# VectorE's block transposes in place of TensorE's six, and the norms' root parts moved into PSUM, in a sliding-window attention and binarised FFN block

## The reference

```python
q, k = l2norm(proj(Wq)), l2norm(proj(Wk))          # 16 heads of 16 channels, norms per head
v = proj(Wv)
attn = q @ k.T                                      # per head
rel = pos[None, :] - pos[:, None]                   # key minus query
mask = (rel < 0) | (rel >= 128)                     # a query sees itself and the next 127 keys
attn = softmax(where(mask, -1e30, attn - abs(rel) * slope[h]))
x = layernorm(x + (attn @ v) @ Wo.T)
h = gelu(x @ binarize(w1).T + b1)                   # 1024 hidden, weights = sign * row mean of |w|
x = layernorm(x + h @ binarize(w2).T + b2)
```

## Time and profile before

| | |
|---|---|
| median of 3 runs | 369.94 us (369.66 to 370.51) |
| span of the profiled execution | 368.4 us |
| PE (TensorE matmul) busy | 353.2 us, 96% |
| DVE (VectorE) busy | 308.7 us, 84% |
| ACT (ScalarE) busy | 307.3 us, 83% |
| POOL (GpSimd) busy | 285.4 us, 77% |
| PE, attention, 107.2 to 135.8 us | 28.60 of 28.60 us |
| granted TensorE clock | 0.997 of full speed over the span |

### The profile page before, as it was taken

One profiled execution on the slowest core, in us unless ns is written; L12 is line 12 of the kernel. 1 busy time (PEld: TensorE's weight loads), 2 busy tenths in 40 slices (PEclk: granted clock), 3 DMA queues, 4 the chain that ended last, 5 costly groups with the idle time before them and its releaser, 6 DMA issues. The chain is left out here.

```text
span 368.4 us, 13096 instructions
## 1 busy us (share of the span) xinstructions
PE 353.2 (96%) x4461; PEld 244.1 (66%) x4461; DVE 308.7 (84%) x771; ACT 307.3 (83%) x532; POOL 285.4 (77%) x440
## 2 busy tenths in 40 slices
PE   8789999999999999999999999999999999999992
PEld 5555676667766776776677677675666667667682
DVE  5977899898898898898899988879777887786775
ACT  3588888898898998898899999988888888887753
POOL 1188999889989999998999999757756856856433
PEclk9999999999999999999999999999999999999998
DMA  7678944744655646667767773303303513413113
GB/s 231 143 117 186 185 109 98 157 99 94 137 120 106 142 96 132 139 159 154 156 144 155 153 147 74 59 4 59 59 0 59 115 45 72 114 39 76 59 59 114
DMA packets 106884, 40.19 MB, mean 109 GB/s; under 512 B 92128, under 2 KB 105824, under 8 KB 106720
## 3 DMA queue, kind: packets, MB, share of 16 engines
q1 hardware_dynamic: 106848, 39.73, 49.6%
HBM read 12.72 MB, written 4.19 MB: 46 GB/s over the span
## 5 line engine op out<-in xcount | busy, mean ns | idle before, releaser
L1341 POOL TENSOR_SCALAR_AFFINE_SELECT prob<-prob 128x512 f32<-128x512 f32 x252 | 153.7, 646 | 11.1 <-ACT prob L700 11.1
L700 ACT ACTIVATE prob<-ps 128x1024 f32<-128x1024 f32 (+1 forms) x128 | 122.2, 1009 | 13.5 <-PE ps L390 13.4
L551 PE MATMUL ps<-yT,sgn 128*128 128x512 f16 x256 | 61.1, 379 | 0.0
L772 ACT ACTIVATE ps<-ps,bias,alpha 128x512 f32<-128x512 f32 x64 | 47.9, 750 | 15.6 <-PE ps L551 12.5
L421 PE MATMUL ps<-wqkv,xt 128*128 128x512 f32 x124 | 58.7, 596 | 1.2 <-DVE qkn L952 1.1
L411 PE MATMUL ps<-prob,vdiag 128*17 128x128 f32 x1024 | 51.3, 274 | 0.3
L411 PE MATMUL ps<-prob,vnext 128*17 128x128 f32 x992 | 49.9, 273 | 0.0
L1409 POOL TENSOR_TENSOR resid<-z,resid 128x256 f32 (+1 forms) x31 | 22.5, 726 | 29.9 <-DVE z L1173 29.9
L551 PEld LDWEIGHTS ps<-yT,sgn 128*128 128x128 f16 x256 | 25.0, 98 | 22.6
L390 PE MATMUL ps<-qkT 64*64 64x192 f16 (+2 forms) x1024 | 33.7, 248 | 2.8 <-DMA qkT<-parts 2.7
L454 PE MATMUL ps<-wo,oT 128*128 128x256 f32 x128 | 36.2, 405 | 0.1
(11 more groups left out here) (113 smaller groups left out, 690.2 us busy)
## 6 DMA issues: line engine op xcount, KB each, us to landing
xt<-in_xT SPq DMA_DIRECT2D x32, 128.0 KB, 2.1
resid<-in_x SPq DMA_DIRECT2D x32, 128.0 KB, 2.2
out_dram<-resid SPq DMA_DIRECT2D x7, 512.0 KB, 2.9
w<-in_w2T SPq DMA_DIRECT2D x1, 1024.0 KB, 7.7
w<-in_w1T SPq DMA_DIRECT2D x4, 256.0 KB, 3.3
w_nat<-in_w SPq DMA_DIRECT2D x4, 256.0 KB, 3.3
wqkv<-in_wqkvT SPq DMA_DIRECT2D x3, 256.0 KB, 3.9
qkT<-parts SPq DMA_TRANSPOSE x39, 4.3
```

Of the source, the lines that this page charges most:

```text
L551: mm = nc.tensor.matmul(ps[:, bank, :], sgn1[:, c, P * k:P * k + P], yT[:, par, a, c, :, :], start=(m == 0), stop=(m == 2 * DC - 1))
L700: nc.scalar.activation(to, scored, ACT.Exp, scale=QK_SCALE ** -2).then_inc(exp_done, 1)
L772: nc.scalar.activation(bank, bank, ACT.Gelu, bias=bias1[:, k:k + 1], scale=alpha1[:, k:k + 1]).then_inc(gelu_done, 1)
L1341: return nc.gpsimd.affine_select(out=at, in_=at, compare_op=ALU.is_ge, fill=0.0, base=-near, pattern=[[0, CH], [1 if near else -1, P]], ch ...
```

## The change

- TensorE's transposes L438 (four) and L445 (two) go, and so do ScalarE's two copies L674 and L680. In their place VectorE turns bank 7 in 32x32 blocks into `turned` in SBUF (`turn_sums`, 512 columns) at the very start of its step, takes the reciprocals and multiplies from `turned` (both inputs are now in SBUF), and turns the 256 columns of `otok` in 32x32 blocks into `oT` (`scale_sums`). The order of the rows of `Wo` is changed on the host to fit.
- `project_out` goes behind `project_qk`, writes to bank 7 and waits for `turn_sums` of the block after; `weighted_sum` waits for `add_output` of that result.
- The root's three temporaries lie in PSUM bank 1 beside the values, from step 4 on (`parts_in_psum`). `project_v` of the next block writes the same bank, so it waits for the Newton round.
- The seeds (L863) go behind `fade_values`. The two products of `fade_values` become one of 512 columns (`faded`).
- The doubling copy goes from VectorE to ScalarE, behind the root.
- GpSimd cuts two chunks at once: four instructions of 1024 columns in a step for eight of 512. The low halves stand between the two pairs.

```diff
+        faded = sb("faded", [P, 2, XS, H, HD + 1])
+        turned = sb("turned", [P, H, 2 * HD])
+        parts_in_psum = tuple(ps[:, VO, D + 64 * n:D + 64 * n + 2 * H + 1] for n in range(3))
...
             def weighted_sum(q, c, slot, near=True):
                 if c == 0:
                     pe.wait_ge(v_ready, q + 2 if near else NB)
-                    count(pe, ot_ready, q)
+                    count(pe, sums_turned, q)
+                    count(pe, resid_done, q - 1 if not isinstance(q, int) or q < NB - 2 else 0)
...
             def project_v(n, slot):
                 count(pe, v_ready, n)
-                count(pe, resid_done, n - 4)
+                if not isinstance(n, int) or 6 <= n < NB - 1:
+                    pe.wait_ge(newton, norm_base(n - 2, True) + NORM_OPS)
...
+            def project_out(q, par):
+                pe.wait_ge(ot_ready, q + 1)
+                pe.wait_ge(sums_turned, q + 2)
                 for k in range(DC):
-                    mm = nc.tensor.transpose(ps[:, OT, P * k:P * k + P], otok[:, P * k:P * k + P], id32[:])
-                mm.then_inc(ot_done, 1)
-            def project_out(q, values, added=0):
-                pe.wait_ge(ot_ready, q + 1)
-                pe.wait_ge(v_ready, values)
-                count(pe, resid_done, added)
-                for k in range(DC):
-                    mm = nc.tensor.matmul(ps[:, VO, D:2 * D], oT[:, k, :], wo[:, k, :],
+                    mm = nc.tensor.matmul(ps[:, OT, D * par:D * par + D], oT[:, par, k, :], wo[:, k, :],
                                           start=(k == 0), stop=(k == DC - 1))
                 mm.then_inc(wo_done, 1)
...
+            def turn_sums(q):
+                dve.wait_ge(pv_done, q + 1)
+                count(dve, onorm_done, q)
+                nc.vector.transpose(turned[:].rearrange("p b d -> p (b d)"), ps[:, OT, :]).then_inc(sums_turned, 1)
+            def scale_sums(q, par):
+                dve.wait_ge(sums_turned, q + 1)
+                nc.vector.reciprocal(rden[:], turned[:, :, HD]).then_inc(rden_done, 1)
+                dve.wait_ge(rden_done, q + 1)
+                count(dve, ot_ready, q)
+                nc.vector.tensor_tensor(otok[:].rearrange("p b a d -> p a b d"),
+                                        turned[:, :, 0:HD].rearrange("p (a b) d -> p a b d", a=2),
+                                        rden[:].rearrange("p (a b) -> p a b", a=2).unsqueeze(3).to_broadcast(
+                                            [P, 2, H // 2, HD]),
+                                        ALU.mult).then_inc(onorm_done, 1)
+                dve.wait_ge(onorm_done, q + 1)
+                count(dve, wo_done, q - 1)
+                nc.vector.transpose(oT[:, par].rearrange("p k t -> p (k t)"),
+                                    otok[:].rearrange("p b a d -> p (b a d)")).then_inc(ot_ready, 1)
...
-                for to, at in ((vdiag, 0), (vnext, 1)):
-                    made = nc.vector.tensor_tensor(to[:, slot, :, 0:HD], v,
-                                                   fade[:, at, :].unsqueeze(2).to_broadcast([P, H, HD]), ALU.mult)
-                made.then_inc(v_ready, 1)
+                nc.vector.tensor_tensor(faded[:, :, slot, :, 0:HD], v.unsqueeze(1).to_broadcast([P, 2, H, HD]),
+                                        fade[:].unsqueeze(3).to_broadcast([P, 2, H, HD]), ALU.mult).then_inc(v_ready, 1)
...
+            def double(n, par):
+                done = n + 1
+                if not isinstance(n, int):
+                    done = act.to_reg(done)
+                act.wait_ge(lo_done, done)
+                nc.scalar.activation(parts[:, par, 0:H, 2:4, :], parts[:, par, 0:H, 0:2, :],
+                                     ACT.Copy).then_inc(parts_ready, 1)
...
-                at = prob[:, NEAR_AT[slot % 2] if near else OWN_AT[slot], CH * c:CH * c + CH, :]
+                at = prob[:, NEAR_AT[slot % 2] if near else OWN_AT[slot], 2 * CH * pair:2 * CH * pair + 2 * CH, :]
                 return nc.gpsimd.affine_select(out=at, in_=at, compare_op=ALU.is_ge, fill=0.0, base=-near,
-                                               pattern=[[0, CH], [1 if near else -1, P]],
+                                               pattern=[[0, 2 * CH], [1 if near else -1, P]],
                                                channel_multiplier=-1 if near else 1)
```

252 lines of the change are left out of this document (112 added, 140 removed).

## The result

| | before | after |
|---|---|---|
| median of the runs, us | 370.23 (369.66 to 372.72, 4 runs) | 376.27 (375.39 to 378.12, 4 runs) |
| ratio | | 1.016, 95% interval 1.012 to 1.020 |
| span of the profiled execution, us | 368.4 | 374.4 |
| mean granted clock | 0.997 | 0.974 |
| PE, DVE, ACT, POOL busy, us | 353.2, 308.7, 307.3, 285.4 | 339.0, 310.9, 293.5, 268.9 |

The kernel became slower by 6.0 us. The forecast was 356.3, and its range ended at 365.2. Here and in the experiments, runs more than 1.5% above the fastest of the same kernel are left out of the medians. TensorE is busy for 14.2 us less, where the forecast's terms for it add to 20.8 (32 x 0.65), and it stands idle for 20.2 us more (35.4 against 15.2). The page of the kernel after says where: its lines 2 are the busy tenths in 40 slices of 9.4 us.

The account below looks back on a forecast made before the run. TensorE's own work was taken to bound the attention step at 7.15 us, three engines close behind. Loop -12.5, edges -2.6 and tail +1.5 gave -13.6 us, a median of 356.3 us; range 349.0 to 365.2.

Parts of the forecast that it names:

- rival (d): VectorE's block transposes cost twice the rate per column; its step becomes 7.40 us, the kernel slower at 380.1 us; 8%.
- rival (b): GpSimd's wide cuts save nothing, 1.24 us each; the round is 6.98 and the time 364.5 us; 12%.
- `otok`'s wait: On VectorE, otok now reads both inputs from SBUF and may wait for a cut: 0.31 us taken, bounds 0 and 1.05.
- rival (c): On VectorE, otok waits about 0.67 us on average behind longer cuts; VectorE's sum is 6.95, the time 365.1 us; 14%.
- The round of pair of cuts, low halves, copy and exponentials: GpSimd's and ScalarE's work tied in a loop by the new order, 6.60 us, 0.10 longer than TensorE's 6.50.
- the forecast's own sign: In the loop, ScalarE idle ahead of the doubling copy, released by the low halves, would show the round; no size given.
- Nothing, with 0.5 to spare: Every fourth block's second transposing DMA lands some 3 us later, at 6.1 in a 6.65 us step, so costs nothing.
- `weighted_sum`'s 0.9 to spare: TensorE reaches weighted_sum at 4.56 us, VectorE ends add_output by 3.7 plus otok's wait, so no cost.
- The rows agree: Claim that step 15's VectorE rows fit the rule: two SBUF inputs contend with GpSimd, at most one does not.
- -0.65: TensorE's saving per step from the removed transposes, booked equally for step 3 and steps 29 to 31.
- -2.6: The edges: steps 3 and 29 to 31 lose 0.65 us each, 2.6 us off in all.
- 1.5 us later: The tail: VectorE gets 3.3 us of transposes with about 1.75 idle, so the FFN starts some 1.5 us later.

Follow-up runs that it names:

- e13: e11 with GpSimd's low halves ahead of both pairs of cuts and ScalarE's doubling copy ahead of the roots: 362.30 us, 0.980 of the kernel before.
- e8: The kernel before with only the change's 1024-column cuts, their waits and GpSimd's order: 390.73 us, ratio 1.056.
- e4: The changed kernel with the doubling copy of steps 4 on moved back from ScalarE to the end of VectorE's step: 390.31 us, 1.058 of the kernel before.
- e9: The changed kernel with all cuts 512 columns and the tail's three first-group high halves moved from VectorE to ScalarE: 367.32 us, 0.993 of before.
- e17: The kernel before with the tail's three high halves moved from VectorE to ScalarE: 370.68 us, ratio 1.001.
- e11: e9 with VectorE's prologue reordered (outputs(0) later) and, in the tail, turn_sums(30) and first_rows moved: 364.06 us, 0.982 of the kernel before.

## Why the prediction was wrong

**What held.** TensorE's part of a step: 6.42 us, forecast 6.50. The prices of VectorE's transposes: 0.717 and 0.446, forecast 0.69 and 0.42 to 0.46, by the rate of the rows next to them. This refutes rival (d), and with it the forecast's estimate of 1.87 us a step worked out from the Trainium skill, page VectorE: DVE Perf Modes, section The three transpose paths; the measured sum is 1.16. The temporaries in PSUM: 0.20 each. The cut: 1.108, forecast 1.05, so rival (b) is out. `otok`'s wait, 0.12 in the mean, forecast 0.31, so rival (c) is out. The round of pair of cuts, low halves, copy and exponentials: the copies follow each other in 6.56 us (123.27 to 129.83), forecast 6.60. Whether that round sets this pace is not shown. By the forecast's own sign ScalarE would stand idle ahead of the copy; it stands idle 0.58 ahead of the roots, for VectorE's seed, and the copy begins 0.03 behind the low halves.

**The loop's gain, 12.0 us for 24 steps forecast, 7.7 measured.** Two steps of the working failed. "Nothing, with 0.5 to spare" for the second transposing DMA had both of its terms too small: the DMAs start 1.8 us behind the step's start and not 0.6 to 1.0, and the scores that wait for the second begin 3.9 us behind its issue (125.92 to 129.79) and not 3. So they wait 1.0 once in four steps, 0.25 a step, and 2.25 ahead of step 28. e13 took most of it away. And `weighted_sum`'s 0.9 to spare was 0.4 too little in the step behind that, where it waits for `add_output`. Neither was the largest error.

**The wide cuts, taken as a saving.** The working priced the cut on GpSimd, which had room (26.41 of 28.60 us), and gave it only one price on VectorE, `otok`'s wait. The rule that the forecast cites was half of it. It says that a VectorE instruction with at most one SBUF input does not contend; the section of the Trainium skill that it names excepts the two-port modes from this. Two kinds with one tensor input, both in SBUF, did wait: the row's `TENSOR_SCALAR` (667 to 1024 ns in e8) and the doubling copy (0.28 to 1.16 in e4). The same section of the Trainium skill, SBUF — State Buffer, section Who interferes with whom, allows for it: copies and tensor-scalar forms can run in a two-port mode and then contend as well, and whoever comes first blocks the other for the whole instruction. The trace of the kernel before had it all. "The rows agree" was read off one step: in the four steps from 107 to 136 us the copy takes 0.34 to 0.71 and the row's instruction 0.41 to 0.86, the norms' seed in step 15 itself takes 0.73 where it takes 0.18 two steps earlier, and `nt_a`, counted as free at 0.20, takes up to 0.62. With a longer cut a wait that is met is longer: `nt_b` went from 530 to 1009 ns, and the free time is 0.20. In the kernel before, that part alone costs 20.6 us (e8), through the Newton round.

**The prologue, which the forecast booked at -0.65.** It cost 6.0 to 6.7. The condition `i >= 4` (`parts_in_psum` from step 4 on) was known: in steps 0 to 3 the temporaries stay in SBUF, where the forecast's own rule makes them wait for a cut of the new length. And `outputs(0)` had grown by two transposes ahead of a product that TensorE waits for. Nothing in a table of the loop shows this; the first 41 us of the timelines do.

**The end, "-2.6" and "1.5 us later".** Without step 3 these add to -0.45. It cost 6.0. The mechanism was named, VectorE falls behind, but it was counted over the last three blocks only, with an idle time of 1.75 us from a stretch of 12. Steps 29 to 31 were booked as if TensorE bound them, at -0.65 each. Over the whole stretch VectorE had 6.1 us idle and got 8.4 more: six pairs of transposes (7.0), the longer waits, less the copy. e9 and e17 show that load counts, by taking work out of it in both kernels, and e11 that the order does.

**The clock.** The forecast had none of it. Where TensorE stood idle for 4.6, 2.25 and 2.7 us, the products behind ran at the lower level. In the prologue that is 1.0 on the projection at 42.75 and 1.4 on the sums at 44.76, 2.4 us on top of an idle time of 4.6.

**The chances.** The slower side had 8%, in one mechanism that did not occur. What did occur was the same kind of wait, in instructions that the working never listed, and at the two ends.
